# Output projection and last layer moved into the block of the heads, with the moments, roots and inverses of two tiles side by side and the first five final sums on GpSimd

## The reference, cut to what matters

```python
x = x + _layernorm(_L0_attn_ref(_layernorm(x, axis=-1), ...), axis=-1)
x = x + _layernorm(_L0_ffn_ref(_layernorm(x, axis=-1), ...), axis=-1)
x = x + _layernorm(_L1_attn_ref(_layernorm(x, axis=-1), ...), axis=-1)
x = x + _layernorm(_L1_ffn_ref(_layernorm(x, axis=-1), ...), axis=-1)
```

## Time and profile before

| | |
|---|---|
| median of 3 runs | 1620.12 us |
| lowest and highest run | 1618.42 and 1624.85 us |
| the profiled execution, its own time | 1626.14 us |
| its span, first to last instruction | 1624.2 us |
| TensorE busy | 1502.8 us, 93% |
| VectorE busy | 1038.6 us, 64% |
| ScalarE busy | 810.8 us, 50% |
| GpSimd busy | 232.0 us, 14% |
| mean granted TensorE clock | 0.961 of full speed |
| in 1547.0 to 1624.2: TensorE, VectorE, ScalarE, GpSimd busy | 63.35, 43.73, 30.66 and 3.18 us |

### The profile page before, as it was taken

One profiled execution on the slowest core, in us unless ns is written; L12 is line 12 of the kernel. 1 busy time (PEld: TensorE's weight loads), 2 busy tenths in 40 slices (PEclk: granted clock), 3 DMA queues, 4 the chain that ended last, 5 costly groups with the idle time before them and its releaser, 6 DMA issues. The chain is left out here.

```text
span 1624.2 us, 22378 instructions
## 1 busy us (share of the span) xinstructions
PE 1502.8 (93%) x8030; PEld 991.4 (61%) x8030; DVE 1038.6 (64%) x2048; ACT 810.8 (50%) x1467; POOL 232.0 (14%) x233
## 2 busy tenths in 40 slices
PE   6867999999999999959979999898999999999987
PEld 4645776666777676647868887786553333333264
DVE  5744666666666666644643433564888999999245
ACT  5325666666666666641221221222117777777834
POOL 2762111112111111100000000001000122331200
PEclk9977999999999999989979999998989999999999
DMA  4142221212122221134212110117420222320001
GB/s 137 53 191 72 85 69 63 69 63 69 63 92 76 69 69 40 34 103 162 97 53 77 59 59 20 52 50 186 148 27 14 72 74 76 77 66 15 18 14 46
DMA packets 63298, 116.83 MB, mean 72 GB/s; under 512 B 12830, under 2 KB 32414, under 8 KB 61902
## 3 DMA queue, kind: packets, MB, share of 16 engines
q1 hardware_dynamic: 59956, 106.63, 20.6%
q10 hardware_dynamic: 3168, 8.65, 2.1%
q0 software_dynamic: 64, 0.11, 0.0%
HBM read 83.04 MB, written 29.66 MB: 69 GB/s over the span
## 5 line engine op out<-in xcount | busy, mean ns | idle before, releaser
L1681 DVE TENSOR_REDUCE ah_minus_half<-ah_ring 128x1 f32<-128x512 f32 x512 | 319.7, 679 | 40.3 <-PE ah_ring L1578 40.0
L968 DVE CUSTOM_DVE_ANT_0 mh_score<-mh_score,mh_mask 128x128 f32<-128x128 f32 (+7 forms) x256 | 195.8, 765 | 179.4 <-PE mh_score L781 179.3
L1641 ACT ACTIVATE ah_probs<-ah_score 128x1024 f32<-128x1024 f32 x256 | 248.7, 1023 | 114.6 <-PE ah_score L1595 113.6
L890 ACT ACTIVATE mh_probs<-mh_score,mh_minus_max 128x128 f32<-128x128 f32 (+7 forms) x256 | 189.6, 741 | 39.8 <-DVE mh_minus_max L968 35.8
L1578 PE MATMUL ah_ring<-ah_k_stack,ah_q_stack 48*128 48x512 f32 x512 | 187.1, 468 | 14.1 <-DVE ah_minus_half L1681 4.2
L1578 PEld LDWEIGHTS ah_ring<-ah_k_stack,ah_q_stack 48*128 48x128 f32 x512 | 82.8, 190 | 176.9 <-DVE ah_minus_half L1681 161.5
L1595 PE MATMUL ah_score<-ah_q_stack,ah_k_stack 49*128 49x512 f32 x512 | 158.1, 445 | 3.8 <-DVE ah_v L1705 2.3
L779 PE MATMUL mh_score<-shared,h_hi 128*128 128x512 f32 (+3 forms) x384 | 152.2, 396 | 3.0 <-ACT mh_probs L890 2.9
L1041 POOL TENSOR_TENSOR h_lo<-mh_pe,h_hi 64x512 fp32r<-64x512 f32 x64 | 81.9, 1279 | 459.0 <-ACT h_hi L876 455.4
L1610 PE MATMUL ah_mix<-ah_probs,ah_v 128*32 128x512 f32 x1024 | 139.0, 615 | 0.6 <-ACT ah_probs L1641 0.6
L781 PE MATMUL mh_score<-shared,h_lo 128*128 128x512 f32 (+3 forms) x384 | 133.0, 346 | 0.0
(11 more groups left out here) (222 smaller groups left out, 2854.7 us busy)
## 6 DMA issues: line engine op xcount, KB each, us to landing
mh_w<-in_w_pairs SPq DMA_DIRECT2D x16, 896.0 KB, 5.6
x<-in_w_inner SPq DMA_DIRECT2D x14, 768.0 KB, 4.1
pe_scratch<-fr_pe_out SPq DMA_DIRECT2D x4, 2048.0 KB, 6.6
mh_pe<-pe_scratch SPq DMA_DIRECT2D x16, 512.0 KB, 4.0
mh_spread<-inverse_scratch SPq DMA_DIRECT2D x64, 128.0 KB, 2.9
a_scratch<-mh_mixed SPq DMA_DIRECT2D x32, 256.0 KB, 2.4
x<-a_scratch SPq DMA_DIRECT2D x8, 1024.0 KB, 6.9
qk_scratch<-ai_ring SPq DMA_DIRECT2D x32, 256.0 KB, 2.7
```

What stands on the lines that cost most here:

```text
L890: nc.scalar.activation(probs[:, s % 2, 0:width], score_ps[s % 2][:, base:base + width], ACT.Exp, bias=minus_max[:, s % 4:s % 4 + 1], scale ...
L968: nc.vector.tensor_tensor_reduce(out=scores, in0=scores, in1=mask[:, S - width:S], scale=-1.0, scalar=3e38, op0=ALU.add, op1=ALU.min, accu ...
L1641: nc.scalar.activation(probs[:, 2 * (u % 2) + c, :], score_ps[c][:].rearrange("p e n -> p (e n)"), ACT.Exp, scale=MHA_SCALE).then_inc(prob ...
L1681: nc.vector.reduce_max(minus_half[:, m:m + 1], ring[:, m % 3, :], AX.X, negate=True).then_inc(max_taken, 1)
```

## The change

The programs of `mha_tail` are no longer a block. It returns five functions, one per engine, and `mha_heads` calls each at the end of that engine's program, in its own block. The banks of PSUM are those that the heads had for the maxima (`ring`) and the scores (`score_ps`). TensorE's program has three waits ahead (`started`). In each step, VectorE takes the moments of Z of tile n - 4 and of Y of tile n one behind the other, then both inverses, and then `hT_lo`; ScalarE takes both roots one behind the other. Each kind has its own row of `stats`. The sum x + zn is on GpSimd for tiles 0 to 4, and on VectorE for tiles 5 to 7, behind `hT_lo`.

In `mha_heads` and `two_layers`:

```diff
-def mha_heads(nc, io, scratch, later, shares, products, place):
+def mha_heads(nc, io, scratch, later, shares, products, place, finish):
...
+        banks = ([ring[:, n, :] for n in range(2)], [score_ps[0][:, n, :] for n in range(2)],
+                 [score_ps[1][:, n, :].rearrange("p (k n) -> p k n", k=ND) for n in range(2)])
+
+        def started(pe):
+            pe.wait_ge(max_taken, TOTAL)
+            pe.wait_ge(bias_in, 32)
+            pe.wait_ge(weights_used, ND)
+
+        finish_sync, finish_gpsimd, finish_tensor, finish_scalar, finish_vector = finish(ctx, banks, started)
         block = ctx.enter_context(nc.Block())
...
             shares.put(sp, GROUPS - 1, 1, out, out_taken)
-            sp.wait_ge(bias_in, 32)
+            finish_sync(sp)
...
+            finish_gpsimd(pool)
...
+            finish_tensor(pe)
...
             take_out(GROUPS - 1, 1)
+            finish_scalar(act)
...
+            finish_vector(dve)
...
-                mha_heads(nc, io, scratch, later, shares, products, place)
-                stage.close()
-                mha_tail(nc, ident, x, later, shares, out_dram, at)
+
+                def finish(ctx, banks, started):
+
+                    return mha_tail(nc, ctx, ident, x, later, shares, out_dram, at, banks, started)
+
+                mha_heads(nc, io, scratch, later, shares, products, place, finish)
```

In `mha_tail`, without the lines that are only moved and indented otherwise:

```diff
-def mha_tail(nc, ident, x, later, shares, out_dram, at):
+def mha_tail(nc, ctx, ident, x, later, shares, out_dram, at, banks, started):
...
-        stats, mv = sb("stats", [P, 2, 6]), sb("mv", [P, 3, NT, 2])
+    stats, mv = sb("stats", [P, 3, 6]), sb("mv", [P, 3, NT, 2])
...
-        py = [ctx.enter_context(nc.psum_tensor(f"at_py{i}", [P, D], F32)) for i in range(2)]
-        pz = [ctx.enter_context(nc.psum_tensor(f"at_pz{i}", [P, D], F32)) for i in range(2)]
-        pt = [ctx.enter_context(nc.psum_tensor(f"at_pt{i}", [P, ND, P], F32)) for i in range(2)]
+    py, pz, pt = banks
...
-        block = ctx.enter_context(nc.Block())
+    BY_POOL = 5
...
+    def gpsimd(pool):
+        shares.divide(pool, GROUPS - 1, 1)
+        for t in range(BY_POOL):
+            pool.wait_ge(z_used, t + 1)
+            nc.gpsimd.tensor_tensor(x[:, t, :], x[:, t, :], zn[:, t % 2, :], ALU.add).then_inc(out_sum, 1)
+            pool.wait_ge(out_sum, t + 1)
...
+        started(pe)
...
         def take_z(t):
-                root(Z, t)
...
         def take_y(t):
-                root(Y, t)
...
         for n in range(STEPS + 1):
             if 0 <= n - 1 < NT:
                 take_x(n - 1)
+            if 0 <= n - 4 < NT:
+                root(Z, n - 4)
+            if n < NT:
+                root(Y, n)
             if 0 <= n - 4 < NT:
                 take_z(n - 4)
...
-                then(nc.vector.bn_stats(stats[:, t % 2, :], source))
+            then(nc.vector.bn_stats(stats[:, kind, :], source))
...
             if 0 <= n - 4 < NT:
-                    t = n - 4
-                    dve.wait_ge(z_ready, t + 1)
-                    moments(Z, t, pz[t % 2][:])
-                    invert(Z, t)
-                    dve.wait_ge(z_used, t + 1)
-                    nc.vector.tensor_tensor(x[:, t, :], x[:, t, :], zn[:, t % 2, :], ALU.add).then_inc(out_sum, 1)
+                dve.wait_ge(z_ready, n - 3)
+                moments(Z, n - 4, pz[n % 2])
             if n < NT:
                 dve.wait_ge(y_ready, n + 1)
-                    moments(Y, n, py[n % 2][:])
+                moments(Y, n, py[n % 2])
+            if 0 <= n - 4 < NT:
+                invert(Z, n - 4)
+            if n < NT:
+                invert(Y, n)
             if 0 <= n - 2 < NT:
                 t = n - 2
                 dve.wait_ge(hT_hi_ready, t + 1)
                 nc.vector.tensor_tensor(hT_lo[:, t % 2, :, :], pt[t % 2], hT_hi[:, t % 2, :, :].bitcast(F32), ALU.subtract
                                         ).then_inc(t_used, 1)
+            if BY_POOL <= n - 4 < NT:
+                t = n - 4
+                dve.wait_ge(z_used, t + 1)
+                dve.wait_ge(out_sum, t)
+                nc.vector.tensor_tensor(x[:, t, :], x[:, t, :], zn[:, t % 2, :], ALU.add).then_inc(out_sum, 1)
             if n < NT:
-                    invert(Y, n)
                 dve.wait_ge(y_used, n + 1)
...
+    return sync, gpsimd, tensor, scalar, vector
```

More of the change, by code:

```diff
@@ L1738, in _ @@
                 shares.invert(dve, b)
-def mha_tail(nc, ident, x, later, shares, out_dram, at):
[L1743 to L1746, removed]
-        stats, mv = sb("stats", [P, 2, 6]), sb("mv", [P, 3, NT, 2])
-        std, rstd, shift = (sb(n, [P, 3, NT]) for n in ("std", "rstd", "shift"))
-        yn, zn, hn = (at(f"at_{n}", [P, 2, D], F32, "down_hi", 2 * D * i) for i, n in enumerate(("yn", "zn", "hn")))
-        hT_hi, hT_lo = (at(f"at_{n}", [P, 2, ND, P], F32R, "down_hi", 2 * D * i) for i, n in ((3, "hT_hi"), (4, "hT_lo")))
-        py = [ctx.enter_context(nc.psum_tensor(f"at_py{i}", [P, D], F32)) for i in range(2)]
-        pz = [ctx.enter_context(nc.psum_tensor(f"at_pz{i}", [P, D], F32)) for i in range(2)]
-        pt = [ctx.enter_context(nc.psum_tensor(f"at_pt{i}", [P, ND, P], F32)) for i in range(2)]
[L1754 to L1759, removed]
-        block = ctx.enter_context(nc.Block())
[L1761 to L1827, removed]
-                root(Z, t)
[L1829 to L1837, removed]
-                root(Y, t)
[L1839 to L1862, removed]
-                then(nc.vector.bn_stats(stats[:, t % 2, :], source))
[L1864 to L1877, removed]
-                if 0 <= n - 4 < NT:
-                    t = n - 4
-                    dve.wait_ge(z_ready, t + 1)
-                    moments(Z, t, pz[t % 2][:])
-                    invert(Z, t)
-                    dve.wait_ge(z_used, t + 1)
-                    nc.vector.tensor_tensor(x[:, t, :], x[:, t, :], zn[:, t % 2, :], ALU.add).then_inc(out_sum, 1)
-                if n < NT:
-                    dve.wait_ge(y_ready, n + 1)
-                    moments(Y, n, py[n % 2][:])
-                if 0 <= n - 2 < NT:
-                    t = n - 2
-                    dve.wait_ge(hT_hi_ready, t + 1)
-                    nc.vector.tensor_tensor(hT_lo[:, t % 2, :, :], pt[t % 2][:], hT_hi[:, t % 2, :, :].bitcast(F32), ALU.subtract
-                                            ).then_inc(t_used, 1)
-                if n < NT:
-                    invert(Y, n)
-                    dve.wait_ge(y_used, n + 1)
-                    nc.vector.tensor_tensor(x[:, n, :], x[:, n, :], yn[:, n % 2, :], ALU.add).then_inc(summed, 1)
-                    dve.wait_ge(summed, n + 1)
-                    moments(X, n, x[:, n, :])
```

113 lines of the change are left out of this document (added).

## The result

The changed kernel takes 1610.38 us (median of 7 runs, 1606.09 to 1613.96) against 1621.86 us (7 runs, 1618.42 to 1624.85) before. The ratio is 0.9926, interval 0.9911 to 0.994: 0.74% faster, 11.5 us between the medians. The forecast was 1606 in 1602 to 1612, a gain of 14.0. The sign and the range held. The gain of 11.5 is 2.5 us short of 14.0 between the medians, but the interval reaches from 9.7 to 14.4 us, so the run times alone do not prove a shortfall. The other 1.7 us between 1610.38 and 1606 are the base: the forecast stood on the median of three runs (1620.12), which with seven runs is 1621.86.

The account below looks back on a forecast made before the run. An engine-to-engine chain, not one full engine, bounds the last layer's end. Hand-over 6.7, +0.1 to the projections' end, 7.4 after, less 0.3 handoffs, taken as 14.0: 1606 us against the 1620.12 median, range 1602 to 1612.

Parts of the forecast that it names:

- Hand-over, 6.7 us: Last mix of the heads to output projection: 4.5 us from an earlier first product, 2.2 from its full clock.
- 5.5 idle us: TensorE's idle time before the first projection product, behind which the prediction saw the clock fall.
- Loop of VectorE and ScalarE under 7.2, TensorE late next: Middle of last layer: loop 8.1 becomes 6.7, TensorE's step of 7.2 then bounds; at most 0.9 gained per step.
- old period of 8.08: Late middle of the old kernel: VectorE's chain per step, rebuilt as 7.8 us, 4% under the measured 8.08.
- Sums on GpSimd beside the lower part: Five final sums on GpSimd, 1.28 us each, mostly beside the lower part: no time cost of their own.
- bound of 0.3: Most that each GpSimd sum may stretch VectorE's work: 0.3 us, 1.5 for five; the forecast took 0.
- The end, 24.0 to 16.6: End of projections to last moments: 24.0 us becomes 16.6, gaining 7.4, with a 0.9 stall and full clock.
- The moved division: GpSimd's division of the last shares: beside one sum of Y, up to 0.8 us, absorbed by three steps' slack.
- Clock rival (0.12): Clock falls at the hand-over anyway or between first projections; one more slow product, 2.2 us: 1608. Chance 0.12.
- The other rivals: VectorE stays bound, 1611.4 to 1613.4 (0.10); slow clock all last layer, 1641 (0.02); hand-over gives nothing, 1612.7 (0.05).
- Contention: GpSimd shares SBUF interfaces with VectorE: two-SBUF-input instructions may stretch, making the result up to 1.5 us later.

Follow-up runs that it names:

- held hand-over: Changed kernel, but TensorE's first projection waits until the last copy of the last shares has landed; one execution, 1619.73 us.
- first profile: First profiled execution of the changed kernel, unedited; 65.1 us from last mix to last moments; that kernel's median 1610.38 us.
- second profile: Profile of the changed kernel run again, unedited; 63.0 us from last mix to last moments; median 1610.18 us, ratio 0.9908.
- tiny: Changed kernel, but GpSimd divides only 8 of the 512 columns of the last half of the last shares; 1608.37 us, ratio 0.992.
- later division: Changed kernel, but GpSimd's division of the last shares waits until VectorE has written the first lower part of hT; 1612.64 us, ratio 0.9927.
- all sums on VectorE: Changed kernel with all eight final sums on VectorE, none on GpSimd; 1613.94 us, ratio 0.9943.
- earlier inverse: Changed kernel with VectorE's inverse of the last sums ahead of the first moments instead of after the first tile; 1612.79 us, ratio 0.9929.

## Why the prediction was right, and where it was off

The mechanism is right in all three parts, and the miss is one term of the sum.

- **Hand-over, 6.7 us.** Right. 5.51 - 1.00 = 4.5 us of gap and 5.57 - 3.38 = 2.2 us of clock; the held hand-over shows that the second follows from the first. The idle time ahead of the first product before was 4.45 us; the prediction's "5.5 idle us" takes in the last mix itself.
- **Loop of VectorE and ScalarE under 7.2, TensorE late next.** Right. The step is 7.2, and VectorE idles 0.44 and 0.72 us ahead of two moments of Y. The terms named for the old period of 8.08 add up to 6.9 to 7.2, not 7.8: two inverses of 0.34 are missing from the list. The forecast does not use that sum.
- **Sums on GpSimd beside the lower part.** Right in cost. GpSimd took 1.26 to 1.30 each; the sums of Y beside it took 0.79 to 1.09 instead of 0.69, once 0.1 over the bound of 0.3, and the slack hid it. What these sums buy was not priced: 2.5 us at the end, the stall of 1.27 instead of 2.05 and the full clock behind it.
- **The end, 24.0 to 16.6.** Right: 1606.22 - 1589.45 = 16.8. The stall was 1.27 where the steps gave 0.9, under the 1.5 named as the limit, and the clock stayed at 1.00 behind it.
- **The moved division, "fully beside one sum of Y; up to 0.8, which three steps of slack 0.5 take up".** This step failed. The sum was hit (1.67, so 1.0 more and not 0.8) and the slack took it. But the change had put Y's inverse ahead of the lower part, and the division's first operation hit the shift in that inverse, where TensorE has no slack. It cost 0.7 us at once and 1.5 more by the clock in the first profile, 0.2 and nothing in the second. The size could be read from the earlier trace rows: the sum ended 0.54 us after GpSimd's operation, and in the kernels here such sums end 0.55 us after it, wherever in it they begin.
- **Clock rival (0.12).** The clock did fall in the first profile, but at neither of the places that the rival names. Behind the hand-over and the gaps of 0.52 and 0.85 it was at 1.00 (1542 to 1558), and it fell behind the 1.57, at a cost of 1.5 instead of 2.2. In the second profile it did not fall. The rule of the Trainium skill (TensorE: Matmul & The Clock Gate, Part 1) that activity releases the throttle fits both profiles and does not tell them apart.
- **The other rivals.** None came: the loop of VectorE stayed under 7.2, the product behind the hand-over took 3.38, and the clock was low once, not through the layer.
- **Contention.** The Trainium skill (GPSIMD Engine Reference, Key points) names VectorE instructions with two SBUF inputs. The trace agrees, for a shift of one column too: its length here is what was left of GpSimd's operation (0.02 us past its end), not its own 0.16 plus a part. The reciprocal just ahead of the shift, of the same size but with one input, kept its 0.16 to 0.17 beside the same multiplication, and the lower part, with one input in PSUM, its 0.68 to 0.69.

The medians moved by 11.5 us in one round and 15.2 in another, and the stretch by 11.9 in one pair of profiles and 14.0 in the other. That leaves open how often each case comes: the spread of the earlier parts hides it in the run times. Of the two causes, the collision is shown (tiny and later division, and the gap that follows the length of the shift in every profile); that a gap of this length brings the clock down rests on one profile of the changed kernel.

## What to carry to other kernels

Joining two stages in one block paid twice here, where TensorE idled between them: the gap (4.5 us), and the slow product behind it (2.2 us). After a reordering, look again at every short instruction that is now ahead of what the full engine waits for, and at what another engine runs at that moment; a one-column operation took up to 1.27 us here. Where run times scatter more than the effect, measure from a landmark inside the profile.

## What the runs showed that was not expected

A VectorE operation of one column, 0.16 us alone, lasted 0.53, 0.82, 1.09 and 1.27 us beside a GpSimd multiplication of 64x512. In every profile in which the two met it ended 0.00 to 0.02 us after GpSimd's operation. The gap of TensorE followed: 0.84 us behind a shift of 0.20, 0.98 behind 0.50, 1.33 behind 0.89, 1.41 behind 0.93 and 1.57 behind 1.09. Where VectorE's sum began first, 0.03 us ahead, it was GpSimd that took 1.82 us instead of 1.26.

The clock fell behind gaps of TensorE of 1.57, 1.80 and 2.05 us, and not behind 1.41 (all sums on VectorE) or 1.33 (held hand-over); behind 1.33 it did fall in the kernel with the earlier inverse, where 0.91 us of idle time stood just ahead of the turn before. The length of one gap alone does not tell.
